# A six-layer attention and feed-forward stage: odd values a slot later, gates first, tables a unit early, key and query products ahead of the turned tiles

## The reference

```python
qkv = x @ Wqkv
q, k, v = jnp.split(qkv, 3, -1)              # 16 heads of 64
q = l2norm(q) * qs
k = l2norm(k) * ksc
q = q * cos * scale + rotate_half(q) * sin * scale
k = k * cos * inv + rotate_half(k) * sin * inv
out = local_attention(q, k, v)               # windows of 32 tokens, each sees itself and the one before
x = out @ Wo + x
...
xn = (x - mu) / jnp.sqrt(var + 1e-05) * g + bln
hg = xn @ W1 + b1
a, gate = jnp.split(hg, 2, -1)
x = a * jax.nn.gelu(gate, approximate=False) @ W2 + b2 + x
```

## Time and profile before

| | us |
|---|---|
| median of 3 runs | 2673.77 |
| lowest, highest | 2671.05, 2684.93 |
| the profiled execution | 2681.69 |
| its span, first to last instruction | 2679.9 |

### The profile page before, as it was taken

The page is one execution under the profiler, slowest core; times in us unless marked ns, Lnnn a source line. Parts: engine busy times, 40 slices in busy tenths (PEclk is TensorE's granted clock), DMA queues, the critical chain, the costliest instruction groups (busy, mean ns, idle before and its releaser), DMA issues. The chain is left out here.

```text
span 2679.9 us, 62181 instructions
## 1 busy us (share of the span) xinstructions
PE 2296.9 (86%) x24591; PEld 1324.1 (49%) x24643; DVE 1401.7 (52%) x3403; ACT 1146.0 (43%) x2573; POOL 913.6 (34%) x807
## 2 busy tenths in 40 slices
PE   4989998799768988888888989897697996998998
PEld 2445666455424555555455545554356443454443
DVE  3544544466367665766666666664364213573333
ACT  1324452155336565656655665654151111263221
POOL 2010000201168676776676766762101002000000
PEclk7989998889689998999999999999696897798999
DMA  2110000000021111111111111110000010000010
GB/s 60 25 29 1 1 1 1 13 6 3 0 65 34 36 38 32 46 29 47 27 40 47 24 43 36 38 24 16 16 3 16 16 31 10 15 2 25 24 36 20
DMA packets 57695, 65.36 MB, mean 24 GB/s; under 512 B 8957, under 2 KB 37285, under 8 KB 57396
## 3 DMA queue, kind: packets, MB, share of 16 engines
q1 hardware_dynamic: 54900, 58.86, 8.6%
q10 hardware_dynamic: 2496, 2.36, 0.4%
HBM read 33.26 MB, written 0.52 MB: 13 GB/s over the span
## 5 line engine op out<-in xcount | busy, mean ns | idle before, releaser
L3348 POOL TENSOR_TENSOR l1fb_rinv<-l1fb_ssq,neghalf 128x8 f32<-128x8 f32 x192 | 316.1, 1647 | 286.2 <-DVE l1fb_ssq L3389 284.6
L3488 ACT ACTIVATE l1fb_p<-ps,l1fb_shift 128x64 f32<-128x64 f32 x768 | 178.6, 315 | 321.9 <-DVE l1fb_shift L3404 180.8
L3539 PE MATMUL ps<-l1fb_wqkv,l1fb_xs 128*128 128x512 f32 x384 | 218.5, 652 | 39.7 <-DVE l1fb_diff L3439 23.6
L3350 POOL TENSOR_TENSOR l1fb_qk<-l1fb_qk,l1fb_r 128x512 f32<-128x512 f32 x192 | 243.8, 1270 | 0.0
L3352 POOL TENSOR_TENSOR l1fb_qk<-l1fb_qk,l1fb_rinv 128x512 f32<-128x512 f32 x192 | 200.7, 1045 | 15.1
L3554 PE MATMUL ps<-l1fb_wqkv,l1fb_xs 128*64 128x512 f32 x384 | 113.9, 674 | 61.0 <-ACT l1fb_kT L3474 56.6
L3397 DVE TENSOR_TENSOR l1fb_r<-ps,l1fb_turn_tab 128x256 f32<-128x256 f32 x384 | 143.0, 414 | 0.0
L3409 DVE RECIPROCAL l1fb_rden<-ps 128x4 f32<-128x4 f32 x192 | 35.0, 182 | 191.5 <-PE ps L3617 191.2
L3387 DVE TENSOR_REDUCE l1fb_ssq<-l1fb_sq 128x8 f32<-128x512 f32 x192 | 129.9, 676 | 8.5 <-ACT l1fb_sq L3468 8.3
L3394 DVE TENSOR_TENSOR l1fb_qk<-ps,l1fb_turn_tab 128x512 f32<-128x512 f32 x192 | 132.7, 691 | 0.3
L3575 PE MATMUL ps<-ident,l1fb_qk 128*128 128x128 f32 x768 | 120.6, 280 | 12.3 <-POOL l1fb_qk L3352 7.1
(11 more groups left out here) (707 smaller groups left out, 5175.2 us busy)
## 6 DMA issues: line engine op xcount, KB each, us to landing
l1fb_v<-l1fb_v SPq DMA_DIRECT2D x48, 260.0 KB
l1fb_v<-l1fb_v SPq DMA_DIRECT2D x48, 195.0 KB
l1fb_wqkv<-in_L_ffn_Wqkv SPq DMA_DIRECT2D x24, 256.0 KB, 2.7
l3f_w<-in_L_ffn_W SPq DMA_DIRECT2D x21, 256.0 KB, 3.0
l2f_w<-in_L_ffn_W SPq DMA_DIRECT2D x16, 256.0 KB, 3.0
l1fb_wqkv<-in_L_ffn_Wqkv SPq DMA_DIRECT2D x6, 512.0 KB, 4.2
l1fb_wo<-in_L_ffn_Wo SPq DMA_DIRECT2D x6, 512.0 KB, 4.0
l1fb_w<-in_L_ffn_W SPq DMA_DIRECT2D x6, 341.0 KB, 2.9
```

The costliest lines, as they stand in the source:

```text
L3348: nc.gpsimd.tensor_tensor(w.rinv[:, u, :], w.ssq[:, u, :], chip.neghalf[:, 0:8], ALU.pow).then_inc(*w.unit_norm.end(f"rinv{u}"))
L3350: nc.gpsimd.tensor_tensor(w.qk[:, u, :], w.qk[:, u, :], w.r2[:, u % 2, :], ALU.add).then_inc(*w.unit_norm.end(f"add{u}"))
L3488: last = nc.scalar.activation(w.p[:, c % 2, q, j, :], ps[:, SCORE_BANK + j, q * SEEN:(q + 1) * SEEN], ACT.Exp, bias=w.shift[:, c, j, q:q + 1])
L3539: nc.tensor.matmul(ps[:, PROJ_BANK(u), :], w.xs[:, x.odd, q * P:(q + 1) * P], w.wqkv[:, col:col + 512], start=True, stop=True)\
```

## The change

- PE: `p8` moves from slot 2 to slot 3, `p9` from slot 3 to the end of slot 5; `p10` and `p11` keep their place. In each slot the query or key product (`p0` to `p7`) stands right behind `T`, ahead of `t` and `V`, where it stood last. In slot 1 `gate'` stands ahead of `V7'`.
- DVE: `r0` stands ahead of `inv7' att7'`. `tab` is in slot 4 and is made one unit earlier, at batch 3, into a new tile `w.next_tab`, for the next layer; the first layer's is made at the start of the stage.
- ACT: a new step `tab` copies `w.next_tab` to `w.turn_tab` (128 x 512) at batch 0, slot 1. `r0` of such a unit waits for it. `xn` is divided: DVE does one operation (`spread` times `g` times the centred tile), ACT adds `bln`, and `gate'` waits for ACT. `c0` stands ahead of `X1`; `v8` and `v9` follow their products.
- `w.r2` has one buffer where it had two: the products of `r_u` wait for POOL's `add(u-1)`, not for `add(u-2)`.
- The order of waits for bank 5 follows: `t7'`, `p8`, `t0`, `t1`, `p9`, `t2`, `p10`, `t3`, `p11`, `t4'`, ...

```diff
-PE_PLAN = """B0 S0 T7' G6' t4' V6' p0 t5' spread'    B1 S1 T0 G7' p1 V7' gate'    B2 S2 G0 p2 V0 T1 t6' p8 value0'    B3 S3 T2 G1 t7' V1 p3 p9 value2'
-             B4 S4 T3 G2 t0 V2 p4 y1    B5 S5 T4 G3 t1 V3 p5 y2' mean    B6 S6 T5 G4 t2 V4 p6 p10 var    B7 S7 T6 G5 t3 V5 p7 p11""".split()
...
+PE_PLAN = """B0 S0 T7' p0 G6' t4' V6' t5' spread'    B1 S1 T0 G7' p1 gate' V7'    B2 S2 G0 p2 V0 T1 t6' value0'    B3 S3 T2 p3 G1 t7' V1 p8 value2'
+             B4 S4 T3 p4 G2 t0 V2 y1    B5 S5 T4 p5 G3 t1 V3 y2' mean p9    B6 S6 T5 p6 G4 t2 V4 p10 var    B7 S7 T6 p7 G5 t3 V5 p11""".split()
...
-        after(eng, w.unit_norm, f"add{(u - 2) % QK}", x.past(0 if u >= 2 else 1))
-        src, r1, r2 = heads(ps[:, PROJ_BANK(u), :]), heads(w.qk[:, u, :]), heads(w.r2[:, u % 2, :])
+        after(eng, w.unit_norm, f"add{(u - 1) % QK}", x.past(0 if u else 1))
+        if u == 0 and x.b == 0:
+            eng.wait_ge(w.tables_in, x.layer + 1)
+        src, r1, r2 = heads(ps[:, PROJ_BANK(u), :]), heads(w.qk[:, u, :]), heads(fp(w.r2))
...
+    def tables(x):
+        if x.b == B - 1 and not (x.j is None and x.layer == FFN_LAYERS - 1):
+            make_tables(x.layer + 1)
+
+    make_tables(0)
...
-        nc.vector.tensor_tensor(fp(w.diff), fp(w.diff), fed(chip, "spread"), ALU.mult).then_inc(*w.made.end("xn0"))
-        after(eng, w.made, "xn0", x)
-        nc.vector.tensor_scalar(fp(w.diff), fp(w.diff), w.col[:, 0:1], w.col[:, 1:2], ALU.mult, ALU.add).then_inc(*w.made.end("xn"))
+        nc.vector.scalar_tensor_tensor(fp(w.diff), fed(chip, "spread"), w.col[:, 0:1], fp(w.diff), ALU.mult, ALU.mult).then_inc(*w.made.end("xn0"))
...
+    def tables(x):
+        if x.b:
+            return
+        eng.wait_ge(w.tables, x.layer * 2 + 1)
+        after(eng, w.rot, "rot7", x.past(1))
+        nc.scalar.activation(w.turn_tab[:, :, :, :, :], w.next_tab[:, :, :, :, :], ACT.Copy).then_inc(w.tables_in, 1)
+
+    def normed(x):
+        after(eng, w.made, "xn0", x)
+        nc.scalar.activation(fp(w.diff), fp(w.diff), ACT.Identity, bias=w.col[:, 1:2]).then_inc(*w.moved.end("xn"))
```

More of the change, by code:

```diff
@@ L3176 @@
 BEHIND = 2
-PE_PLAN = """B0 S0 T7' G6' t4' V6' p0 t5' spread'    B1 S1 T0 G7' p1 V7' gate'    B2 S2 G0 p2 V0 T1 t6' p8 value0'    B3 S3 T2 G1 t7' V1 p3 p9 value2'
-             B4 S4 T3 G2 t0 V2 p4 y1    B5 S5 T4 G3 t1 V3 p5 y2' mean    B6 S6 T5 G4 t2 V4 p6 p10 var    B7 S7 T6 G5 t3 V5 p7 p11""".split()
[L3185 to L3188, removed]
+PE_PLAN = """B0 S0 T7' p0 G6' t4' V6' t5' spread'    B1 S1 T0 G7' p1 gate' V7'    B2 S2 G0 p2 V0 T1 t6' value0'    B3 S3 T2 p3 G1 t7' V1 p8 value2'
+             B4 S4 T3 p4 G2 t0 V2 y1    B5 S5 T4 p5 G3 t1 V3 y2' mean p9    B6 S6 T5 p6 G4 t2 V4 p10 var    B7 S7 T6 p7 G5 t3 V5 p11""".split()
+DVE_PLAN = """max0 inv6' att6' r7'    xn' max1 r0 inv7' att7'    max2 inv0 att0 r1    g0' g1' max3 inv1 att1 r2
+              g2' max4 inv2 att2 r3 tab    x1 max5 inv3 att3 r4    x2' centre max6 inv4 att4 r5    vareps max7 inv5 att5 r6 diag""".split()
+ACT_PLAN = """X0 e4' c7' q0 e5'    tab c0 xn' X1 q1 gelu0' gelu1' gelu2'    X2 c1 q2 e6'    X3 c2 e7' q3 v8
+              X4 c3 e0 q4    X5 shift c4 e1 q5 v9    X6 dsq c5 e2 q6 v10    X7 c6 e3 q7 v11 xs""".split()
 POOL_PLAN = """n7'    n0    n1    n2    n3    n4    n5    root n6""".split()
@@ L3229, in l1_ffn_layers @@
         w.att_made = lasting(chip, "attended", each("att", ITEMS))
[L3230 to L3231 removed]
+        w.norm, w.moved = Steps(sem("norm"), ["x1", "diff", "vareps", "diag"]), Steps(sem("moved"), ["x1s", "dsq", "xn"])
+        w.made = Steps(sem("made"), ["xn0", "g0", "g1", "g2", "x2"])
         w.sqs, w.turned, w.vals = Steps(sem("sqs"), each("sq", QK)), Steps(sem("turned"), each("e", 8)), Steps(sem("vals"), [f"v{u}" for u in range(8, 12)])
@@ L3349, in unit_norm @@
         after(eng, w.rot, f"rot{u}", x)
-        nc.gpsimd.tensor_tensor(w.qk[:, u, :], w.qk[:, u, :], w.r2[:, u % 2, :], ALU.add).then_inc(*w.unit_norm.end(f"add{u}"))
+        nc.gpsimd.tensor_tensor(w.qk[:, u, :], w.qk[:, u, :], fp(w.r2), ALU.add).then_inc(*w.unit_norm.end(f"add{u}"))
         after(eng, w.unit_norm, f"add{u}", x)
@@ L3368, in l1_ffn_dve, with make_tables @@
     eng.wait_ge(w.ready, 2)
[L3370 to L3373, removed]
+    def make_tables(layer):
         for k in range(2):
@@ L3377, in tables @@
                 o = slice(0, DH) if part == 0 else slice(DH // 2 - lo, DH - lo)
-                last = nc.vector.tensor_tensor(w.turn_tab[:, k, part, :, o], f.xpos[:, k, part, :, o],
-                                               f.spread[:, k, x.layer, lo:hi].unsqueeze(1).to_broadcast([P, QT, hi - lo]), ALU.mult)
+                last = nc.vector.tensor_tensor(w.next_tab[:, k, part, :, o], f.xpos[:, k, part, :, o],
+                                               f.spread[:, k, layer, lo:hi].unsqueeze(1).to_broadcast([P, QT, hi - lo]), ALU.mult)
         last.then_inc(w.tables, 1)
-        eng.wait_ge(w.tables, x.layer + 1)
+    def tables(x):
+        if x.b == B - 1 and not (x.j is None and x.layer == FFN_LAYERS - 1):
+            make_tables(x.layer + 1)
+    make_tables(0)
     def rotate(x, u):
@@ L3520, in squares @@
         nc.scalar.activation(w.g[:, 2, :], fp(w.diff), ACT.Square).then_inc(*w.moved.end("dsq"))
-    l1_ffn_run(eng, ACT_PLAN, {"q": PROJECT, "e": PROJECT, "v": PROJECT, "xs": 2, "shift": FEED, "dsq": FEED, "gelu": FEED},
-               {"q": square, "e": turned, "v": values, "X": weights, "c": kept, "gelu": gelu, "xs": next_input, "shift": residual_moved, "dsq": squares})
+    l1_ffn_run(eng, ACT_PLAN, {"q": PROJECT, "e": PROJECT, "v": PROJECT, "xs": 2, "shift": FEED, "dsq": FEED, "gelu": FEED, "tab": PROJECT, "xn": FEED},
+               {"q": square, "e": turned, "v": values, "X": weights, "c": kept, "gelu": gelu, "xs": next_input, "shift": residual_moved, "dsq": squares,
+                "tab": tables, "xn": normed})
 def l1_ffn_pe(nc, eng, chip, f, w):
@@ L3545, in odd_window @@
             eng.wait_ge(w.v_in, x.layer * 16 + 16)
[L3546 to L3549, removed]
+        if m:
+            after(eng, w.turned, f"e{m}", x)
         else:
-            after(eng, w.turned, f"e{m}", x)
+            after(eng, w.turned, "e7", x.past(1))
         weights = w.wqkv[:, 2 * H * DH:3 * H * DH].rearrange("p (c j d) -> p j c d", j=2, d=DH)
@@ L3560, in turn @@
         after(eng, w.unit_norm, f"qk{even + 1}", x)
-        before = {0: "v9", 3: "v10", 4: "v11"}
+        before = {0: "v8", 2: "v9", 3: "v10", 4: "v11"}
         if n in before:
             after(eng, w.vals, before[n], x)
[L3565 to L3569, removed]
         else:
             after(eng, w.turned, f"e{n - 1}", x)
+        if n == 6:
+            after(eng, w.gelu, "gelu2", x.past(2))
         for c in range(2):
@@ L3674, in gates @@
         now = x.past(-2)
-        after(eng, w.made, "xn", x)
+        after(eng, w.moved, "xn", x)
         eng.wait_ge(w.w1_in, x.layer * 16 + 16)
```

11 lines of the change are left out of this document (6 added, 5 removed).

## The result

The changed kernel takes 2658.99 us in the median of 4 runs (2656.94 to 2662.42), the kernel before 2675.27 (2671.05 to 2684.93, 4 runs). The ratio is 0.9935 with a 95% interval of 0.9906 to 0.9965, so 9 to 25 us less. The forecast was 24.8 us less. The profiled execution of after takes 2662.42 us, its span 2659.2, against a span of 2679.9 before: 20.7 us less. The two profiled executions lie 6.4 and 3.4 us above the medians of their runs, so the spans show some 4 us more of a gain than the medians' 16.3.

What follows compares the result with a forecast made beforehand. PE's queue bounds the kernel, with a 2.89 us wait at `p8` and low clock behind it. 37.8 us of work plus new waits gives 43.6 against 44.35 per ordinary unit; 24.8 less overall gives 2649 us, range 2632 to 2670.

Steps and rivals of the forecast that it cites:

- the low clock behind it: PE after the 2.89 us wait at `p8` in slot 2: clock at half level, costing 1.6 us, expected to go.
- The base of 37.8 us of PE work: Ordinary unit: 44.35 less 4.9 of waits and 1.6 of low clock leaves 37.8 us at full clock, same in both kernels.
- The waits of the ordinary unit: Nine or so PE waits after the change, 0.2 to 1.2 us each, 5.9 us together against 4.9 before; unit 43.6.
- the 6.5 us from `V0` to `p8`: Slots 2 and 3: two chains in sequence take 6.5 us against 5.3 of PE work, so `p8` waits 1.2.
- ACT's part: Second half of `xn'`, moved from DVE to ACT: 0.43 us, hidden beside `p1`.
- The tables: `tab` on DVE in slot 4 beside POOL: 1.03 to 5 us; nothing lost at 2.95, about 1 us at 5.
- Units of other kinds: Loop-start units gain 1.2 us each, batch 3 units 2.0; over units 2 to 22 all units gain 24.8.
- The first two units and the tail: Stage's start and end: gaps of other kinds, counted at nothing, one us either way.
- (1): Rival, chance 0.08: the clock still falls once a unit, 1.6 us in 21 units, about 30 us; program 2679.
- (2): Rival, chance 0.05: the clock falls twice a unit, at `p1` and `p8`, 27 us more; program 2706.
- (3): Rival, chance 0.07: waits read as bare are covered as `att` comes sooner; unit 42.5, program 2626.
- (4): Rival, chance 0.13: waits half a us longer per unit, batch 3 units gain 1 us only; program 2664.

## Why the prediction was right, and where it was off

**What binds.** PE's queue, its one large wait and the low clock behind it: right. Filling that wait, which leaves PE no less to do, gave 1.55 us a unit, and the prediction had 1.6. As forecast, PE waits longer than before (5.57 us at nine places) and the unit's gain is the clock.

**The base of 37.8 us of PE work.** 43.24 less the nine waits, 5.57, is 37.67. Right within 0.15.

**The waits of the ordinary unit.** Forecast against measured: `p0` 0.45 and 0.37, `t5'` 0.3 and 0.30, `spread'` 0.2 and none, `p1` 0.96 and 0.76, `p8` 1.2 and 1.10, `y1` and `y2'` 0.96 and 0.89 each, `p10` 0.45 and 0.57, `p11` 0.4 and 0.32. Each is within 0.2 in this unit; the one at the loop's start has 0.33 at `p1` and no wait at `p0` and `t5'`. One was missing: `p2`, 0.37, since the gates first put `V7'`, and so `att7'`, late, and `G0` waits for it. The sum was 43.6 and is 43.24. The method behind it was to take each chain as one spacing of the trace and to set PE's own work against it, and it held: the 6.5 us from `V0` to `p8` is 6.48.

**`xn`, tables, `r2`.** ACT's part takes 0.51 and not 0.43. Timeline of after, ACT's part in unit 12, then DVE's tables beside POOL in unit 14:

```profile
1313.57 0.51 ACT L3516 ACTIVATE l1fb_diff<-l1fb_diff,l1fb_col 128x256 f32<-128x256 f32 x1
```

```profile
1423.62 2.10 DVE L3375 TENSOR_TENSOR l1fb_next_tab<-l1f_xpos,l1f_spread 128x128 f32<-128x128 f32 x6
```

The tables took 2.10 us, inside the 1.03 to 5 of the prediction, and hid: batch 3 has the ordinary pitch, 43.65 against the 43.8 forecast. ACT's copy takes 0.63, against 0.6. Single `r2` showed no wait on PE. No run tried it apart.

**Units of other kinds.** In units 12 to 15 the loop's start gained 1.35 against 1.2, batch 3 2.18 against 2.0, ordinary 1.11 against 0.75. Units 2 to 22 gave 30.5 us and not 24.8: 10.7 and not 9.0 in the ordinary ones and those before a jump, 12.6 and not 11 in batch 3, 7.2 and not 4.8 at the loop's start. The four there gained between 0.3 and 3.4 us each, so that unit 14 came so near its forecast is luck.

**The term that failed** is the sentence "The first two units and the tail have gaps of other kinds; I count them at nothing, one us either way". They cost 11.3 us: 5.8, 2.0 and 3.5. The units gave 5.7 us more than forecast and the later stages 1.7, and that hid half and more of it; the forecast came as near as it did by misses that partly cancel. In unit 0 fewer steps of the units before are there to fill PE. Timeline of after in unit 0, one turn of a loop that runs through three engines: `V2`, `att2`, `r3`, then `p5`, which waits for `r3`, and, behind a turned tile, `V3`:

```profile
803.04 0.46 PE L3627 MATMUL ps<-l1fb_v,l1fb_both 64*32 64x65 f32 x32
...
803.91 0.42 DVE L3418 TENSOR_TENSOR l1fb_att<-ps,l1fb_rden 128x256 f32<-128x256 f32 x1
...
805.65 0.75 DVE L3401 TENSOR_TENSOR l1fb_r<-ps,l1fb_turn_tab 128x256 f32<-128x256 f32 x2
...
806.45 1.99 PE L3554 MATMUL ps<-l1fb_wqkv,l1fb_xs 128*128 128x512 f32 x2 [1.38 <-DVE l1fb_r L3401]
...
809.23 0.68 PE L3627 MATMUL ps<-l1fb_v,l1fb_both 64*32 64x65 f32 x32
```

and of PE in before, `V2` and `V3` of the same unit:

```profile
801.18 0.46 PE L3617 MATMUL ps<-l1fb_v,l1fb_both 64*32 64x65 f32 x32
...
804.14 0.46 PE L3617 MATMUL ps<-l1fb_v,l1fb_both 64*32 64x65 f32 x32
```

With the product behind `V3`, a wait for DVE's `r3` doesn't hold `V3`. Ahead of it, it does, and the next `r` depends on `V3`. From `V2` to `V3` it is 6.19 us in after (803.04 to 809.23, at half clock from the product on) and 2.96 before. Putting only `p4` and `p5` back gave 3.0 us of it; with the products ahead and nothing else unit 0 is 39.12, 6.8 above before. The odd values later cost 2.1 more by themselves there (34.47, in the kernel with that move alone). With all products last it still is 35.69, at a clock of 0.90, so the order isn't all of the 5.8. The tail's 3.5 us were seen but not taken apart. They aren't the order's: from the last `B0` to the next stage's first product it is 66.4 us before, 65.8 with the products ahead alone, 65.4 with the odd values alone, 69.9 in after and 71.0 with the products last. What differs is when the clock falls: `y1`, which meets the full clock before, meets the lower level after.

**The rivals.** (1) and (2), the clock falling once or twice a unit, are out: 1.00 in units 12, 13, 15 and 20. (3), the waits covered, is out: they stand where they were summed. (4), 2664, is the nearest in its number, 5 us off, but not in its mechanism: the waits were shorter, not longer, and batch 3 gained in full. What was lost against the forecast stands at the stage's ends. What the prediction had no rival for is the one that the runs show to be the main thing: the change is a large gain, 3.2%, with one part in it that takes 2.5% back. The prediction's own rows had both terms, 2.9 + 1.6 gained at `p8` and 0.96 + 0.96 + 1.2 + 0.6 and more lost at bare waits.

The parts, in the ordinary unit: before 44.35; the odd values later 40.61; the rest but the products 39.96; the products ahead 43.24.
